# Spreading B with one fp32 matmul of 16 rows instead of one bf16 matmul of three parts

## What is computed

```python
# layer 0, per 7x7 window: 6 heads of 32 channels
xn = layernorm(x); q, k, v = xn @ qkv_w + qkv_b
x = x + softmax(q k^T * scale) v @ proj_w + proj_b
x = x + gelu(layernorm(x) @ w1 + b1) @ w2 + b2
# layer 1, per image and direction: 16 states n per channel
dt, B, C = split(x_proj(xs)); dt = softplus(dt_proj(dt) + bias)
h[t] = exp(dt[t] * A) * h[t-1] + (dt[t] * x[t]) * B[t]
y[t] = sum over n of h[t] * C[t]
# then the four directions are summed, and a last layernorm
```

## Time and profile before

| | us |
|---|---|
| median of 2 runs | 23,726.78 |
| profiled execution, its own time | 23,592.88 |
| span of its instructions | 23,590.9 |
| the three merged stretches together | 15,226 |
| mean granted TensorE clock over the span | 0.719 |

### The profile page before, as it was taken

How to read it: one execution, slowest core, us unless ns; L and a number is a source line. 1 busy time by engine, 2 the same in 40 slices (tenths; PEclk the granted TensorE clock), 3 DMA queues, 4 the chain that set the end, 5 groups by cost and what they waited for, 6 DMA issues and landing times. The chain is left out here.

```text
span 23590.9 us, 324977 instructions
## 1 busy us (share of the span) xinstructions
PE 19474.3 (83%) x96064; PEld 7726.4 (33%) x96064; DVE 19105.3 (81%) x23738; ACT 10774.5 (46%) x20618; POOL 17745.1 (75%) x14036
## 2 busy tenths in 40 slices
PE   8987888898887988989988788899988867777731
PEld 5532333333332333333333233333333211111111
DVE  5557888888876888888887688888888689999976
ACT  3344555545544445444454455544455434444420
POOL 0036888888874788888786688887788489999977
PEclk9986777666778667666678777666667876777665
DMA  0034455444545445444454545444444455555556
GB/s 18 14 130 124 96 103 103 97 95 96 103 106 168 89 98 100 95 95 92 91 102 131 145 96 100 98 96 96 90 98 97 161 128 123 119 117 120 121 134 167
DMA packets 1323235, 2508.72 MB, mean 106 GB/s; under 512 B 88168, under 2 KB 1066832, under 8 KB 1306224
## 3 DMA queue, kind: packets, MB, share of 16 engines
q1 hardware_dynamic: 1321584, 2489.33, 48.1%
HBM read 1981.62 MB, written 507.38 MB: 106 GB/s over the span
## 5 line engine op out<-in xcount | busy, mean ns | idle before, releaser
L1859 POOL TENSOR_TENSOR m_pr<-m_hs,m_c_u 128x448 f32<-128x448 f32 x8064 | 9048.1, 1136 | 2579.5 <-DVE m_hs L1742 2137.5
L1377 PE MATMUL m_psum<-m_pr,m_red 128*64 128x224 f32 x32256 | 6414.3, 501 | 221.0 <-ACT m_y_sb L1558 151.9
L1722 DVE TENSOR_TENSOR m_psum<-m_psum,m_u_u 128x448 f32<-128x448 f32 x5040 | 3094.2, 614 | 2231.0 <-PE m_psum L1367 2210.1
L1742 DVE TENSOR_TENSOR_SCAN m_hs<-m_da_t,m_carry,m_psum 128x448 f32<-128x448 f32 x4320 | 4790.2, 1128 | 37.6 <-ACT m_da_t L1572 29.6
L1841 POOL TENSOR_TENSOR m_dbp<-m_u_u,m_bp_u 128x448 f32<-128x448 f32 x3024 | 3424.7, 1133 | 112.2 <-DMA m_c_u<-scr_bc 112.2
L1367 PE MATMUL m_psum<-m_br_u,m_sel 48*128 48x448 bf16 x5040 | 2343.6, 465 | 1235.5 <-DVE m_hs L1742 1085.8
L1572 ACT ACTIVATE m_da_t<-m_dt_u,m_a_neg 128x448 f32<-128x448 f32 x5040 | 3257.7, 657 | 54.8 <-DMA m_c_u<-scr_bc 53.5
L1377 PEld LDWEIGHTS m_psum<-m_pr,m_red 128*64 128x64 f32 x32256 | 2171.1, 175 | 2802.6 <-issue 1636.3
L1742 DVE TENSOR_TENSOR_SCAN m_hs<-m_psum,m_carry,m_dbp 128x448 f32<-128x448 f32 x2592 | 2948.5, 1138 | 0.7
L1133 POOL TENSOR_TENSOR c_pr<-c_hs,c_c_u 128x784 f32<-128x784 f32 x1536 | 2803.7, 1847 | 189.6 <-DVE c_hs L1097 189.6
L1040 ACT ACTIVATE c_psum<-c_dt_u,c_a_neg 128x784 f32<-128x784 f32 x1536 | 1410.4, 918 | 2147.9 <-DVE c_hs L1097 2116.5
(11 more groups left out here) (176 smaller groups left out, 26030.8 us busy)
## 6 DMA issues: line engine op xcount, KB each, us to landing
m_c_u<-scr_bc SPq DMA_DIRECT2D x672, 896.0 KB
m_dt_u<-scr_dt SPq DMA_DIRECT2D x672, 336.0 KB
m_u_u<-scr_u SPq DMA_DIRECT2D x672, 336.0 KB
m_bp_u<-scr_bc SPq DMA_DIRECT2D x672, 336.0 KB
c_c_u<-scr_bc SPq DMA_DIRECT2D x128, 1568.0 KB, 26.8
scr_dt<-p_dt_o SPq DMA_DIRECT2D x128, 1176.0 KB, 4.5
scr_u<-p_u_o SPq DMA_DIRECT2D x128, 1176.0 KB, 5.5
c_dt_u<-scr_dt SPq DMA_DIRECT2D x128, 588.0 KB, 7.4
```

Of the source, the lines that this page charges most:

```text
L1377: mm = pe.matmul(Y[64 * h:64 * h + 64, :], red[:], pr[:, s % RP, HT * h:HT * h + HT], start=(p == 0 and opens(w)), stop=(p == NPR - 1))
L1722: nc.vector.tensor_tensor(slot(s), slot(s), u_u[:, d, s // NPR, :], ALU.mult).then_inc(mul_done, 1)
L1742: nc.vector.tensor_tensor_scan(hs[:, s % RH, way], decay(w, s)[:, way], data, init, ALU.mult, ALU.add).then_inc(scan_done, 1)
L1859: nc.gpsimd.tensor_tensor(pr[:, s % RP, :], hs[:, s % RH, :], c_u[:, d, s % NPR, :], ALU.mult).then_inc(prod_done, 1)
```

## The change

B is spread from its fp32 rows. `sel` becomes 16 rows of fp32, loaded straight from DRAM, and ScalarE's conversion goes. `br_u` becomes 16 rows of fp32, loaded from `scr_bc`. The matmul of L1367 is written as before, but both operands are now fp32. The count of `a_done` falls from three to two. The preparation stage still writes the three parts, which the last scan stage goes on using. The order of the instructions on each engine is the same, but for the one activation that goes.

```diff
-        sel = sb("sel", [3 * NS, NPR, 128], BF16)
+        sel = sb("sel", [NS, NPR, 128])
...
-        br_u = sb("br_u", [3 * NS, 2, CT], BF16)
+        br_u = sb("br_u", [NS, 2, CT])
...
-            for dst, src in ((pr[0:3 * NS, 0:3, :].rearrange("p a t -> p (a t)")[:, 0:NPR * 128].rearrange("p (a t) -> p a t", a=NPR), sel_h),
+            for dst, src in ((sel[:], sel_h[0:NS]),
...
-                sp.dma_start(br_u[:, d, :], bps[at, d, :, :, t].rearrange("u k n t -> (u k n) t")).then_inc(u_in[d], 16)
+                sp.dma_start(br_u[:, d, :], bcs[at, 32 * d:32 * d + NS, t].rearrange("u n t -> (u n) t")).then_inc(u_in[d], 16)
...
-            pe.wait_ge(a_done, 3 * ROUND)
+            pe.wait_ge(a_done, 2 * ROUND)
...
-            nc.scalar.activation(sel[:], pr[0:3 * NS, 0:3, :].rearrange("p a t -> p (a t)")[:, 0:NPR * 128].rearrange("p (a t) -> p a t", a=NPR),
-                                 ACT.Copy).then_inc(a_done, 1)
             nc.scalar.activation(a_neg[:], a_neg[:], ACT.Exp).then_inc(a_done, 1)
-            act.wait_ge(a_done, 3 * ROUND - 1)
+            act.wait_ge(a_done, 2 * ROUND - 1)
...
-            act.wait_ge(a_done, 3 * ROUND)
+            act.wait_ge(a_done, 2 * ROUND)
...
-            pool.wait_ge(a_done, 3 * ROUND)
+            pool.wait_ge(a_done, 2 * ROUND)
```

## The result

The changed kernel takes 29,047.35 us (median of 2 runs, 29,030.93 to 29,063.78) against 23,726.78 before. The ratio is 1.224, with a 95% interval from 1.215 to 1.234. The forecast was 28,150 us in a range from 26,700 to 30,000: the direction and the kind of loss were right, and about 900 us of it were missing. The measured time lies somewhat nearer to the third rival (29,800 us) than to the forecast.

A forecast was written before the change was run, and what follows sets the result against it. TensorE, fullest in the merged stretches, was taken to set the pace: 4,580 - 1,090 + 970 - 3 = +4,457 us on the profiled execution gave 28,050, and with run offset 28,150 us, range 26,700 to 30,000.

The forecast's parts named there:

- the third rival: Merged stretches: the clock falls further, to 0.60, as long thin products break up dense stretches; 29,800 us, chance 0.17 with its tail.
- The wait for scans before the spread: TensorE before L1367 in the merged stretches: its 1,085.8 us wait for scans to free a PSUM slot goes, -1,090 us.
- The fp32 price: L1367's 5,040 spreads: fp32 adds 1.16 us each at clock 0.50 and 0.59 at 1.00, +4,580 us of TensorE time.
- the fit 0.88 = a + 224b, 2.78 = a + 784b: From L1374 and L1439 at clock 0.50: fixed part 0.12, 0.00339 per column, so 1.64 us for a 448-column fp32 spread.
- the 970 of the term: Merged stretches: mean clock falls from 0.69 to 0.655, so 18,122 us of TensorE work becomes 19,090, +970 us.
- The clock that keeps its 0.69: Merged stretches: mean clock stays 0.69, leaving only the fp32 price less the covered scan wait; 27,080 us, chance 0.20.
- The clock at 1.00 throughout: Merged stage: a fuller TensorE holds 2.4 GHz and VectorE becomes the bound; some 21,700 us, chance 0.03.
- The small edits: `sel` conversion goes, -3 us; the changed `br_u` load is nil, with 0 to 50 us either way.

## Why the prediction was right, and what it missed

**TensorE was the engine to watch.** One reading was off without harm: in the 40 slices of the earlier trace rows the clock goes from 0.52 to 0.97, not from 0.66 to 0.99. For the rest right: its slack in the merged stage went, and its work then set the pace. The wait for scans before the spread, costed at 1,090 us, is gone: the idle time before L1367 fell from 1,235.5 to 181.2 us. In all TensorE's idle time fell by 1,221 us, 131 more than the term.

**The fp32 price.** The kind was right (two records, rows do not matter to the duration), the size too small. 5,040 x (0.56 x (1.79 - 0.48) + 0.44 x (0.94 - 0.29)) is 5,140 us against the 4,580 of the sum: 560 us were missing. The step that failed is the fit 0.88 = a + 224b, 2.78 = a + 784b. An fp32 product pays one fixed extra when the product before it cuts the array differently, and another before the next product starts when that one does. The spread stands before a reduction and, on 16 rows, pays both. Each of the two rows at 0.50 in the earlier trace rows pays only one of them: L1374 stands directly behind L1439, a product over the full array too, and so paid nothing for its start; that L1439 stands behind a reduction but before L1374, and so paid nothing at its end. The same two lines stand in the kernel before among other neighbours:

```profile
5057.31 1.12 PE L1374 MATMUL m_psum<-m_y_sb,m_same 128*128 128x224 f32 x2
5058.36 1.02 PE L1377 MATMUL m_psum<-m_pr,m_red 128*64 128x224 f32 x4
...
5098.14 2.98 PE L1439 MATMUL m_psum<-m_h2T,m_w_sb 96*128 96x392 f32 x4
5101.06 0.55 PE L1367 MATMUL m_psum<-m_br_u,m_sel 48*128 48x448 bf16 x1
```

Here L1374 stands behind attention's small products and L1439 before a spread, so each pays both extras, and they take 1.05 and 2.92 us. The same fit, 1.05 = a + 224b and 2.92 = a + 784b, gives b = 0.00334 and a = 0.30, so 1.80 us for 448 columns, and 1.79 were measured. The price per column was right, and the fixed part was put at 0.12 instead of 0.30 us.

**The clock.** The mechanism was the one forecast, the size was not. The mean is 0.61 and not 0.655. What is left of TensorE's added time, 6,692 - 5,140 = 1,550 us, stands against the 970 of the term: 580 us more. The formula behind the term (work x 0.69/clock) was rough as well: from 13,427 + 5,140 us it would give 21,000 us at 0.61, and 20,118 were measured. It overstates what a lower clock costs, since a part of the distances between products does not scale with it, nor do the waits (a bf16 spread takes 0.48 us at 0.50 and 0.29 us at 1.00, which is more than half). It was luck that this made up for a part of the other two errors: with the right clock of 0.61 in it, the term would have been 18,122 x 0.69/0.61 - 18,122 = 2,380 us and the sum 29,460, above the measured time although the price was 560 us short. The three differences, 560 + 580 - 131, are the 1,010 us between the 28,050 of the sum and the span of 29,062.

**The rivals.** The clock that keeps its 0.69 (27,080 us) did not come. Run with 48 rows, though, the fp32 product does have 0.69, and takes 27,502 us. The clock at 1.00 throughout (21,700 us) did not come either, and its reason is refuted: TensorE was 98% busy at 0.61. The Trainium skill ("TensorE: Matmul & The Clock Gate", Part 1) ties the clock to how busy TensorE has been; here 98% went with 0.61, 91% with 0.96 (fp32 on 128 rows) and 84% with 0.83 (bf16 on 128 rows). The rival's arithmetic held all the same: once the padding brought the clock to 0.96, TensorE's time (13,193 us) fell to near VectorE's (12,634 us), and the kernel took less than the one before. The fp32 spread did not become free by that: on the same 128 rows it costs 938 us more than the bf16 one. The further fall to 0.60 (29,800 us) was the nearest of the rivals, nearer than the forecast in the clock and in the time. I had it as the less likely case, because I thought the large MLP products would hold the clock up; they did so in fewer stretches.

**The small edits.** Nothing of them shows. Outside the merged stretches the time is what it was: the last scan and the output take 5,254 us against 5,257 before.

## What to carry to other kernels

A narrow product is not cheaper in time than a wide one, and if there are many of them, it can also keep the granted clock down for everything else; before changing a product's type or splitting it, look at how many rows it fills and at the clock of the stretch it runs in. Where the contraction is short and the clock is at 0.50 much of the time, padding it with zero rows adds next to no instructions (it zeroes two buffers once per stage) and was worth 6.7% here. When a price is fitted from two rows of a trace, take two whose neighbours on both sides are of the kind that the new product will have.

## What was not expected of the hardware

- The rows of one product moved the mean clock of the whole stage: 0.61, 0.69 and 0.96 for the same fp32 spread on 16, 48 and 128 rows, that is 29,047, 27,502 and 23,031 us, and the added rows were zeros. The Trainium skill ("TensorE: Matmul & The Clock Gate", the table "Why this matters for your kernels") says that a product on 32 rows takes the same time as one on 128; the price of a single one agrees, 0.94 and 0.95 us at 1.00 behind a product of another cut, and the effect on the clock comes on top.
- A fully busy TensorE does not have the full clock: 98% busy at 0.61.
- An fp32 product over the full array took 0.84 us behind a product of the same cut and 0.95 us behind one that uses half of the columns. The product behind matters too: L1439 at 0.50 took 2.78 us before a product over the full array and 2.92 us before a spread on 48 rows.
